# The third pass of a two-layer transformer kernel: who writes the high part of the MLP's first product

## The reference

```python
# layer 0 (pass 0 of the kernel)
tgt = tgt + self_attn(layer_norm(tgt), mask) + (memory @ Wg.T + bg)
x   = tgt + relu(layer_norm(tgt) @ W1.T + b1) @ W2.T + b2
# layer 1 (passes 1 and 2)
x = mha(ln1(x), ln1(x), causal=True) + x           # pass 1
y = mha(ln2(x), encoded, causal=False) + x         # pass 2
y + relu(ln3(y) @ mlp_w1 + mlp_b1) @ mlp_w2 + mlp_b2
```

## Time and profile before

| | |
|---|---|
| three timed runs | 1516.74, 1516.67, 1515.88 us; median 1516.67 us |
| the profiled execution | 1518.18 us, of which the span from first to last instruction is 1516.4 us |
| granted TensorE clock, mean | 0.989 of full speed |
| busy: PE / PEld / DVE / ACT / POOL | 93% / 77% / 77% / 69% / 55% |
| passes in the span | pass 0 to about 600 us, pass 1 to about 1010 us, pass 2 after that |
| a step of the third pass | 32.3 us: the wait of the third MLP piece ends at 1034.67 us in step 34 and at 1422.23 us twelve steps later |

### The profile page before, as it was taken

How to read it: one execution, slowest core, us unless ns; L and a number is a source line. 1 busy time by engine, 2 the same in 40 slices (tenths; PEclk the granted TensorE clock), 3 DMA queues, 4 the chain that set the end, 5 groups by cost and what they waited for, 6 DMA issues and landing times.

```text
span 1516.4 us, 39426 instructions
## 1 busy us (share of the span) xinstructions
PE 1411.4 (93%) x13620; PEld 1164.5 (77%) x13620; DVE 1163.5 (77%) x3860; ACT 1040.2 (69%) x2104; POOL 833.7 (55%) x1138
## 2 busy tenths in 40 slices
PE   6889999999999999998888888889999999999987
PEld 5679989988998988876666676657777777777757
DVE  3888888888888888778788778777777776777653
ACT  4777777777777776666666666676666677676663
POOL 4455555555555565655555545545665656665532
PEclk8999999999999999999999999999999999999999
DMA  6454443344434434444554555563344333444200
GB/s 179 146 153 128 126 112 112 113 116 121 127 113 112 121 115 121 143 126 131 162 161 130 154 158 144 154 170 107 106 127 136 100 113 105 114 130 127 77 29 15
DMA packets 161589, 187.09 MB, mean 123 GB/s; under 512 B 15984, under 2 KB 136176, under 8 KB 161392
## 3 DMA queue, kind: packets, MB, share of 16 engines
q1 hardware_dynamic: 161104, 183.78, 42.4%
q10 hardware_dynamic: 288, 0.79, 0.2%
HBM read 125.78 MB, written 58.72 MB: 122 GB/s over the span
## 4 chain that ended last, share of the span: by engine, by line
PE 70%; DVE 12%; issue 7%; ACT 7%; POOL 3%; DMA 1%; SPq 1%; ACTq 0%; DVEq 0%; POOLq 0%
PE d_ps L514 28%; PE o_ps L664 9%; PE d_ps L817 9%; PE s_ps L586 7%; PE t_ps L600 7%; PE t_ps L634 4%; DVE prob L1049 3%; PE m_ps L521 2%; ACT q_stack L879 2%; DVE o_q L1137 1%; ACT prob_t L871 1%; ACT h_f L979 1%; DVE top L1034 1%; ACT xt_hi L888 1%; PE m_ps L681 1%
## 5 line engine op out<-in xcount | busy, mean ns | idle before, releaser
L871 ACT ACTIVATE prob_t<-t_ps 128x384 f32<-128x384 f32 (+1 forms) x512 | 276.1, 547 | 258.3 <-PE t_ps L634 150.4
L586 PE MATMUL s_ps<-k_stack,q_stack 96*128 96x256 bf16 (+1 forms) x1536 | 284.8, 267 | 36.0 <-DVE top L1049 23.5
L862 ACT ACTIVATE prob<-prob,neg_max 128x256 f32<-128x256 f32 x512 | 230.9, 505 | 64.8 <-DVE neg_max L1049 61.8
L1291 POOL TENSOR_TENSOR h_lo<-h_f,h_hi 128x512 fp32r<-128x512 f32 x124 | 159.4, 1285 | 112.9 <-DVE h_hi L1181 102.8
L1049 DVE CUSTOM_DVE_ANT_0 prob<-s_ps,bias_sb 128x256 f32<-128x256 f32 x512 | 194.5, 417 | 30.3 <-PE s_ps L586 28.2
L586 PEld LDWEIGHTS s_ps<-k_stack,q_stack 96*128 96x128 bf16 x1536 | 115.8, 98 | 127.8 <-issue 51.2
L1034 DVE TENSOR_REDUCE top<-s_ps 128x2 f32<-128x512 f32 x256 | 170.4, 681 | 49.4 <-PE s_ps L586 47.9
L634 PE MATMUL t_ps<-q_stack,k_stack 108*128 108x256 bf16 (+1 forms) x1024 | 201.6, 264 | 4.1 <-ACT q_stack L879 4.1
L1049 DVE CUSTOM_DVE_ANT_0 prob<-s_ps,causal 128x128 f32<-128x128 f32 (+1 forms) x512 | 156.9, 351 | 46.9 <-PE s_ps L586 46.1
L664 PE MATMUL o_ps<-prob_t,v_sb 128*17 128x256 f32 (+1 forms) x3072 | 192.0, 368 | 0.0
L600 PE MATMUL t_ps<-ident_sb,prob 128*128 128x128 f32 x1024 | 155.9, 274 | 1.3 <-DVE prob_t L1247 1.2
(11 more groups left out here) (155 smaller groups left out, 4012.5 us busy)
## 6 DMA issues: line engine op xcount, KB each, us to landing
parts<-q_part SPq DMA_DIRECT2D x96, 192.0 KB, 2.3
parts<-k_part SPq DMA_DIRECT2D x96, 192.0 KB, 2.3
q_stack<-parts SPq DMA_DIRECT2D x96, 192.0 KB, 3.3
k_stack<-parts SPq DMA_DIRECT2D x94, 192.0 KB, 3.3
q_stack<-parts SPq DMA_DIRECT2D x96, 128.0 KB, 3.1
k_stack<-parts SPq DMA_DIRECT2D x94, 128.0 KB, 3.2
ct_kept<-ct_hl SPq DMA_DIRECT2D x16, 512.0 KB, 3.4
x_in<-x_mid SPq DMA_DIRECT2D x32, 256.0 KB, 3.6
```

The lines of the kernel that those rows point to most:

```text
L586: last = mm(s_ps[:, h % 2, q * S:q * S + n], q_stack[0:ROWS, t.par, head_of(t, h), q * P:(q + 1) * P], k_stack[0:ROWS, t.par, head_of(t, h ...
L862: last = nc.scalar.activation(prob[:, h % 4, q, :], prob[:, h % 4, q, :], ACT.Exp, bias=neg_max[:, h % 4, q:q + 1], scale=-1.0)
L871: nc.scalar.activation(prob_t[:, h % 8, 0:n], t_ps[:, h % 2, 0:n], ACT.Exp, scale=-1.0)\
L1291: g.tensor_tensor(dst, a, b, ALU.subtract).then_inc(done, 1)
```

## The change

In the steps of kind 2 ScalarE issues four ACTIVATE instructions for a piece in place of two: two write `h_hi` from PSUM and signal `h_h`, and two write `h_f` and signal `h_done`. VectorE's cast is left out in these steps. GpSimd's subtraction waits for `h_done` in place of `h_h`, and ScalarE no longer waits for `h_h` of piece `n - 2`. Pass 0 (but for its last task, whose MLP is in step 17) and step 47 keep the cast. The name `H_ON_ACT = (2,)` lists kinds, not passes.

```diff
+H_ON_ACT = (2,)
...
+        self.h_on_act = self.tail or self.end or self.kind in H_ON_ACT
...
                     act.wait_ge(w1_mm.sem, w1_mm.after(st.old, n + 1))
                     if n >= 2:
-                        if not (st.tail or st.end):
+                        if not st.h_on_act:
                             act.wait_ge(h_h.sem, h_h.after(st.old, n - 1))
                         act.wait_ge(h_l.sem, h_l.after(st.old, n - 1))
-                    for f in range(2 if st.tail or st.end else 0):
+                    for f in range(2 if st.h_on_act else 0):
                         c = C_B1 + FT * MLP.index(st.old.p) + 2 * n + f
                         last = nc.scalar.activation(h_hi[:, 2 * n + f, :], mlp_bank(st, n)[:, f * S:(f + 1) * S],
                                                     ACT.Relu, bias=cols_sb[:, c:c + 1])
-                    if st.tail or st.end:
+                    if st.h_on_act:
                         last.then_inc(h_h.sem, 1)
...
-                if h - 2 in st.w1_at and has(st.old, MLP) and not (st.tail or st.end):
+                if h - 2 in st.w1_at and has(st.old, MLP) and not st.h_on_act:
                     n = st.w1_at.index(h - 2)
                     dve.wait_ge(h_done.sem, h_done.after(st.old, n + 1))
                     v.tensor_copy(h_hi[:, 2 * n:2 * n + 2, :], h_f[:, n % 2]).then_inc(h_h.sem, 1)
...
-                    if st.tail:
+                    if st.h_on_act:
                         pool.wait_ge(h_done.sem, h_done.after(st.old, n + 1))
                     else:
                         pool.wait_ge(h_h.sem, h_h.after(st.old, n + 1))
```

## The result

The changed kernel is slower: 1524.1 us against 1516.74 us (medians of five runs each), a ratio of 1.0049 with a 95% interval of 1.0035 to 1.0063. The forecast was 1523.0 us. The profiled execution took 1522.7 us, with a span of 1520.9 us.

What follows compares the result with a forecast made beforehand. The prediction took TensorE, busy 97.76 of 100 us in the third pass, as the bound, so only its waits count. 13 x 0.46 + 0.3 = 6.3 us gave a median of 1523.0 us, range 1520.3 to 1527.5 us.

Steps and rivals of the forecast that it cites:

- +0.72 at the third piece: Slot 7: ScalarE's new pair stands ahead of piece 0's h_done, so TensorE's third MLP piece starts 0.72 us later.
- hidden pair: Rival: TensorE's slot 7 start bound by something else, so only part of 0.72 us appears; 1516.7 to 1519.5 us; chance 0.07.
- +0.04 at the fourth piece: Slot 8: ScalarE finishes piece 1 slightly after TensorE could start the fourth MLP piece, adding 0.04 us.
- -0.30 in slot 11: Slot 11: without piece 2's cast, VectorE's reduction starts earlier and TensorE's wait for scores shrinks from 0.34 to 0.04 us.
- the other three: The step's casts besides piece 2's: no TensorE wait for VectorE follows them, so leaving them out was costed at nothing.
- 0.46 us a step: Third pass: the net delay left in each of 13 steps after the slot 7, 8 and 11 terms.
- The value projection's margin of 0.13 us: Slot 11: the value projection needs all four h_done at 1235.19 and comes at 1235.32, so passes with 0.13 us to spare.
- Step 17, +0.3: Step 17: third piece delayed 0.72, partly absorbed at the score wait and the flip's wait; +0.3 us, between 0 and 0.7.
- The total: Whole kernel: 13 x 0.46 + 0.3 = 6.3 us slower, median 1523.0 us, slower by 0.4%.
- ScalarE as the bound: Rival: ScalarE bounds slots 7 to 11, pairs cost 0.80 to 0.85 us, no payback; 1527.6 us; chance 0.21.
- VectorE's relief pays it back: Rival: fewer casts also win back the 0.4 us lost at the flip; 0.04 us a step, 1517.2 us; chance 0.08.
- The price of a cast: VectorE's h_hi casts: 0.43 us each, so the 56 that go are 24 us of VectorE.

Runs made afterwards that it cites:

- piece_0_on_act: Against the changed kernel: ScalarE writes h_hi of piece 0 only, pieces 1 to 3 keep VectorE's cast; step 32.97 us, median 1527.59 us.
- cast_left_out: Against the changed kernel: ScalarE's h_hi pair left out too, so nobody writes h_hi in kind 2 steps; step 31.95 us, median 1512.09 us.
- piece_2_on_act: Against the changed kernel: ScalarE writes h_hi of piece 2 only, other pieces keep VectorE's cast; step 31.95 us, median 1512.13 us.
- pair_added_cast_kept: Against the kernel before: ScalarE also writes h_hi ahead of h_f in kind 2 steps, VectorE still casts; step 33.07 us, median 1528.79 us.
- pieces_2_3_and_early: Against the kernel before: ScalarE writes h_hi of pieces 2 and 3 and takes piece 0 out at slot 6's head; median 1508.34 us.
- piece_2_and_early: Against the kernel before: ScalarE writes h_hi of piece 2 only and takes piece 0 out at slot 6's head; median 1508.06 us.
- change_piece_0_early: Against the changed kernel: ScalarE takes piece 0 out of PSUM at slot 6's head; step 32.53 us, median 1521.44 us.

## Why the prediction was right, point by point

- **+0.72 at the third piece** is 0.77: a pair of 0.73 us ahead of `h_done`, paid in full, and 0.04 us because ScalarE starts on piece 0 only 0.37 us ahead of the scores of slot 7, where it was 0.41. piece_0_on_act has it nearly alone (+0.67 a step). So the rival of a hidden pair is out. The earlier trace rows shows the third piece's wait 14 times; the gap of 0.04 us behind `h_f` was read in one step only.
- **+0.04 at the fourth piece** is 0.09; piece 1's pair makes it. In the traced step the scores of slot 8 come 1.72 us after the third piece, where it was 1.75, so 0.83 us are left at the fourth piece, where the prediction had 0.76.
- **-0.30 in slot 11** is -0.32, and cast_left_out measures the casts' whole worth at 0.35 us a step. That the other three are worth nothing in the third pass is shown by piece_2_on_act, whose step is the same.
- **0.46 us a step** is 0.44. In the traced step 0.49 us are left between the scores of slot 7 and those of slot 11 (6.73 us before, 7.22 after), so some 0.05 us come back in other slots. The value projection's margin of 0.13 us was 0.15, and it never waited for `h_f`.
- **Step 17, +0.3**, was mis-sized: it is 0.8. Two things failed there. I let the flip's wait of 0.24 us absorb part of the delay, but `x_in` comes out of VectorE's queue behind `o_q`, which itself waits for TensorE, so it moved along: pair_added_cast_kept has 649.89 - 589.20 = 60.69 us in this stretch, +0.74, with its wait of 0.26 us intact. And the two casts left out on that way (pieces 2 and 3, 0.30 and 0.34 us) were eaten by `o_n`, 0.67 us longer. In the third pass this lengthening is there too (1.71 us in the traced step), and hidden: pieces_2_3_and_early, which has it, has a step of 31.62 us, and piece_2_and_early, which has not, 31.61.
- **The total** comes to 13 x 0.44 + 0.8 = 6.5 us; the prediction had 6.3. That it is so near is luck in part: the step was put 0.02 us too high, 0.3 us in all, and step 17 0.5 us too low. The medians show 7.4 us, with an interval of 5.3 to 9.6 us (0.35% to 0.63% of 1516.7). The 0.26 us lost in pass 1 after step 17, and gone again by step 34, were in no term of mine, and I have no experiment on them.
- **ScalarE as the bound** did not happen in the change: a pair costs 0.73 us and not 0.80 or more. In change_piece_0_early its sign is there, a wait for `h_f` at the fourth piece. The range is said to hold most of this rival, but it ends at 1527.5 us, below the rival's own 1527.6.
- **VectorE's relief pays it back** failed as argued: the flip's wait for `tf_a` hardly moved, from 4.8 to 4.5 us in 12 waits, with four casts less in a step.
- **The price of a cast**, 0.43 us, is the median of the earlier trace rows, and long ones count too: the casts take 29.2 us less in the changed kernel (below), 0.52 us for each of the 56 and not 0.43. Since only piece 2's 0.30 us counted, the time does not hang on it.
- **The Trainium skill's rule**, page "ScalarE: Activation LUTs", section "Rules for kernel authors", that a relu belongs on VectorE, gives the right sign for the change as a whole. It does not decide here: the relu into `h_hi` on ScalarE in place of VectorE's cast is worth -0.35 us a step for piece 2 and costs 0.67 for piece 0. No run has the relu itself on VectorE, so what the page says of its price is not tested.

## What to carry to other kernels

Price moved work by what stands behind it in its new queue, piece by piece: two instructions of 0.73 us together cost 0.67 us at one slot and won 0.35 us at another of the same loop, while both engines had a quarter of their time idle or more. Before moving work to another engine, look whether the waiting engine's item can be issued earlier in the queue that it is in; here that was worth as much as the best move, and the two add. After mending one wait, trace the queue again, since the next limit may be one slot away.

## What the runs showed of the hardware that I had not expected

VectorE's `o_n` (a tensor_tensor of 128x256 with both inputs in SBUF) takes 0.42 us when GpSimd is idle and up to 1.38 us (1.46 in step 17 of the changed kernel) when GpSimd's subtraction of 128x512, 1.29 us long, is under way. The tile's instructions from 1100 to 1400 us, in piece_2_on_act and then in the changed kernel (ns min/median/max):

```profile
L1131 DVE TENSOR_TENSOR o_n<-o_q,rden x20: 416/422/425, 1103.6 to 1391.7; 128x256 f32<-128x256 f32 x20
```

```profile
L1126 DVE TENSOR_TENSOR o_n<-o_q,rden x18: 411/894/1379, 1108.0 to 1371.1; 128x256 f32<-128x256 f32 x18
```

The Trainium skill, page "SBUF — State Buffer", section "Who interferes with whom", says that a VectorE instruction with two SBUF inputs contends with a GpSimd instruction that reads SBUF. The trace agrees: of the pair in the step above, which starts at 1238.89, the first took 1.38 us and the second, with GpSimd's subtraction over, 0.41. The first ends at 1240.27, 0.29 us after the subtraction (1238.69 to 1239.98). The same distance, 0.28 us, comes back where the first `o_n` starts into a subtraction in step 17 of the kernel before, the changed one, cast_left_out and pieces_2_3_and_early, with `o_n` at 0.79, 1.46, 0.71 and 1.48 us. So in these places what is paid is the rest of the subtraction, and not a fixed price. VectorE's cast of piece 1 in the kernel before looks alike, at twice its usual length; it ends at 1230.52, 0.28 us after the subtraction of the earlier trace rows, but no run was made to test that:

```profile
1229.65 0.87 DVE L1181 CAST h_hi<-h_f 128x512 fp32r<-128x512 f32 x1 [0.19 <-ACT h_f L979]
```

So taking work off VectorE let GpSimd's work start earlier, and VectorE paid for it in `o_n`: 1.71 us for the pair in this step, 1.07 before. The groups of VectorE's instructions over the whole span (busy us, mean ns), in the kernel before and in the changed one:

```profile
L1181 DVE CAST h_hi<-h_f 128x512 fp32r<-128x512 f32 x120 | 69.9, 583 | 17.9 <-ACT h_f L979 17.7
L1124 DVE TENSOR_TENSOR o_n<-o_q,rden 128x256 f32<-128x256 f32 x64 | 30.0, 509 | 1.1
```

```profile
L1183 DVE CAST h_hi<-h_f 128x512 fp32r<-128x512 f32 x64 | 40.7, 635 | 2.0 <-ACT h_f L981 2.0
L1126 DVE TENSOR_TENSOR o_n<-o_q,rden 128x256 f32<-128x256 f32 x64 | 39.1, 650 | 1.1
```

The casts take 29.2 us less and `o_n` takes 9.1 us more, a third of what was won. The prediction had VectorE's busy time 25 us lower from the casts alone. It is 18.5 us lower: 29.2 less 9.1, and 1.6 us more in other groups, which I did not follow.
